# First four tiles of the first layer as fp32 products, and a last batch pooled with queries on the partitions

## The reference

```python
# layer 0, per batch, with the expert of the batch
h = gelu(x @ fc1_w.T + fc1_b)                     # 512 -> 2048, exact gelu
y = concat([h @ fc2_w.T + fc2_b,                  # 384 shared outputs
            h @ experts_w[idx].T + experts_b[idx]])  # 128 outputs of the expert
x = x + y
# layer 1
s = tanh(x @ W1 + b1) @ v                         # one score per token
# mask by the batch's type: l <= j, l >= j, or l != j
p = softmax(where(mask, s[None, :], -1e30), -1)   # 512 x 512
x = x + (p @ x) / mask.sum(-1)[:, None]
```

## Time and profile before

| what | us |
|---|---|
| median of three runs | 1385.22 |
| profiled execution | 1384.67 |
| its span, first to last instruction | 1382.8 |
| TensorE busy | 1355.1 (98%) |
| VectorE busy | 1208.0 (87%) |
| ScalarE busy | 853.2 (62%) |
| SP's queue of DMAs | 61.90 MB, 13.3% of 16 engines |

### The profile page before, as it was taken

The page is one execution under the profiler, slowest core; times in us unless marked ns, Lnnn a source line. Parts: engine busy times, 40 slices in busy tenths (PEclk is TensorE's granted clock), DMA queues, the critical chain, the costliest instruction groups (busy, mean ns, idle before and its releaser), DMA issues.

```text
span 1382.8 us, 21714 instructions
## 1 busy us (share of the span) xinstructions
PE 1355.1 (98%) x8666; PEld 862.6 (62%) x8666; DVE 1208.0 (87%) x2025; ACT 853.2 (62%) x1471; POOL 0.2 (0%) x4
## 2 busy tenths in 40 slices
PE   6989999999999999999999999999999999999997
PEld 2437658485675847557484665847567484765855
DVE  6788589988888988889988888988889898888998
ACT  4776837568383765828467483765928467483753
POOL 0000000000000000000000000000000000000000
PEclk9999999999999999999999999999999999999999
DMA  7141002020100202001020200202011020200001
GB/s 257 36 178 62 1 23 69 1 84 9 62 31 16 78 1 77 16 31 62 9 84 1 69 24 16 77 0 77 16 46 48 16 77 1 77 16 16 16 18 46
DMA packets 29623, 63.82 MB, mean 46 GB/s; under 512 B 5970, under 2 KB 6610, under 8 KB 27090
## 3 DMA queue, kind: packets, MB, share of 16 engines
q1 hardware_dynamic: 29090, 61.90, 13.3%
q10 hardware_dynamic: 432, 0.53, 0.1%
HBM read 45.64 MB, written 16.78 MB: 45 GB/s over the span
## 4 chain that ended last, share of the span: by engine, by line
PE 92%; DVE 4%; ACT 2%; issue 0%; DVEq 0%
PE ps L469 44%; PE ps L398 40%; PE ps L485 4%; PE ps L351 2%; DVE raw L160 1%; PE ps L493 1%; ACT hh L169 1%; PE ps L666 1%; ACT w2h L169 1%; DVE cl L166 0%; ACT xl L1004 0%; DVE w1l L166 0%; DVE xr L160 0%; PE ps L776 0%; DVE raw L509 0%
## 5 line engine op out<-in xcount | busy, mean ns | idle before, releaser
L469 PE MATMUL ps<-hh,w2h 128*128 128x512 f16 x768 | 291.8, 380 | 0.0
L469 PE MATMUL ps<-hh,w2l 128*128 128x512 f16 x768 | 291.8, 380 | 0.0
L469 PE MATMUL ps<-hl,w2h 128*128 128x512 f16 x768 | 291.6, 380 | 0.0
L398 PE MATMUL ps<-xh,w1h 128*128 128x256 f16 x960 | 261.7, 273 | 0.3 <-DVE xl L166 0.3
L398 PE MATMUL ps<-xl,w1h 128*128 128x256 f16 x960 | 261.7, 273 | 0.0
L398 PE MATMUL ps<-xh,w1l 128*128 128x256 f16 x960 | 261.7, 273 | 0.0
L441 ACT ACTIVATE g<-ps,b1s,ds 128x512 f32<-128x512 f32 x240 | 173.9, 775 | 101.6 <-PE ps L398 101.6
L160 DVE TENSOR_TENSOR raw<-raw 128x512 f32<-128x512 f32 (+2 forms) x324 | 219.9, 699 | 1.0 <-issue 0.2
L509 DVE TENSOR_TENSOR_SCAN raw<-raw 128x512 f32<-128x512 f32 x180 | 213.2, 1213 | 0.0
L398 PE MATMUL ps<-xh,ch 128*128 128x256 f16 x720 | 196.4, 273 | 0.0
L398 PE MATMUL ps<-xl,ch 128*128 128x256 f16 x720 | 196.3, 273 | 0.0
(11 more groups left out here) (162 smaller groups left out, 2009.5 us busy)
## 6 DMA issues: line engine op xcount, KB each, us to landing
out<-xr SPq DMA_DIRECT2D x63, 256.0 KB, 2.4
xr<-in_xT SPq DMA_DIRECT2D x62, 256.0 KB, 2.9
er<-in_ew SPq DMA_DIRECT2D x15, 1024.0 KB, 5.6
raw<-in_w SPq DMA_DIRECT2D x32, 256.0 KB, 7.7
er<-in_w SPq DMA_DIRECT2D x3, 1024.0 KB, 10.1
xr<-in_ew SPq DMA_DIRECT2D x1, 1024.0 KB, 5.7
xr<-in_xT ACTq DMA_DIRECT2D x2, 256.0 KB, 4.8
aws<-in_aw SPq DMA_DIRECT2D x1, 256.0 KB, 8.6
```

The costliest lines, as they stand in the source:

```text
L398: r = e.matmul(half_bank(*to), w, m, start=i in (1, 5) and c == 0 and n == 0, stop=c == 1 and n == 2, skip_group_check=True)
L469: m = e.matmul(out_bank, w, h[:, k, :], start=False, stop=k == NH - 1 and i == 2, skip_group_check=True)
```

## The change

Start of batch 0:

- Tiles 0 to 3 of the first layer are computed as fp32 products of unsplit w1 and x (`plain`), in an order by arrival; their GELUs take scale 1.0 and write to `g` and not over w1. 36 small products on ones precede everything. Bounds of w1 tiles 0 to 5 and x are taken before the first scale; those of tiles 6 to 9 come behind the low parts of x.
- The splits of w1 tiles 0 to 3, which later batches need, move behind tiles 5 and 6 and to output block 0. w1 tiles 4 to 15 are reloaded one by one in the loop, tiles 0 to 3 not at all; x of batch 1 is loaded before the loop. h parts 0 and 1 are made before the loop. The bound of w2's second block moves into the loop, the expert's bound and scale from output block 1 to block 0, w2's third bound to (0, 2). The load of w2's third block is issued last.

Last batch:

- The pooling of batch 14 stops ahead of the last four operations of its last block; they are issued behind the weights' sum.
- Scans read the scores in PSUM, without the masks' constants, which are added in the two following maxima; one masked copy of the scores is left, and its second half waits for a scan.
- x (natural layout) is copied once more, unsplit, to `xn`. In the products the weights are stationary and nh, nl moving: queries are on the partitions, and the output is in token layout, put in order on the host side together with the transposition that was there. The fourth query tile is in two pieces of 256 columns.
- Totals: three adds of the four weight rows on VectorE, then four one-column fp32 products; count, product and reciprocal are 128x4. Evacuation is one operation per piece. Idle products: 17 and not 22.

```diff
+    def plain(k, cs=range(KD)):
+        if 0 in cs:
+            bank_of[k] = turn()
+        n, free = bank_of[k]
+        for c in cs:
+            fc1_done[0, k] = PE.op(lambda e, c=c: e.matmul(pf[n], w1r[k][:, c * P:(c + 1) * P], xr[:, 0, c, :], start=c == 0, stop=c == KD - 1),
+                                   w1_ready[k], x_ready[0, c], *free)
...
+    warm(36)
     w1_biggest(0)
     biggest(x5[:, 0, 0:1], xr[:, 0, 0, :], x_ready[0, 0])
     w1_biggest(1)
...
+    w1_biggest(2, 3, 4, 5)
+    w_max = w1_column(0, 3)
...
     def first_batch():
-        fc1(0)
+        for k, cs in ((0, (0, 1)), (1, (0, 1)), (0, (2, 3)), (1, (2, 3)), (2, (0, 1, 2))):
+            plain(k, cs)
+        sx_ready[0] = t = chain_scale(xc(0), w1c + 3, chain_sum(xc(0), w1c + 3, w_max, x_max))
+        plain(2, (3,))
+        plain(3)
+        fc1_scale(0, 2, 3, t)
+        split_w1_high(4, t)
+        x_hi = [split_x0_high(0)]
         gelu(0)
+        x_hi += [split_x0_high(c) for c in (1, 2, 3)]
         gelu(1)
+        split_w1_high(5, t)
+        gelu(2)
+        split_x0_low(0, x_hi[0])
         split_w1_low(4)
+        for c in (1, 2, 3):
+            split_x0_low(c, x_hi[c])
+        w1_biggest(6, 7, 8, 9)
+        first["pairs"] = t
         t = w1_column(3, 5)
         gelu(3)
         fc1(4, (0, 1))
         summed = chain_sum(w1c + 3, w1c + 5, t)
...
-        done = 0
+        for j in (0, 1):
+            high(0, j)
+            low(0, j)
+        for c in range(KD):
+            load_x(1, c)
+        done = 2
...
+                reload_w1([j] if j >= PLAIN else [])
             done += 2
             if k >= 12:
                 split_w2(0, 0, k - 12)
-        load_w2(2, 0, w2s_ready[0, 3])
-        big = one_bound(w2c + 1, 0, er[:, 1, :], w2_ready[1])
+            if k == 14:
+                big = one_bound(w2c + 1, 0, er[:, 1, :], w2_ready[1])
...
+        load_w2(2, 0, w2s_ready[0, 3])
...
+        if (o, j) == (0, 0):
+            first["expert"] = one_bound(ec(0), 2, expert_rows(0), e_ready[0])
...
-            reload_w1(range(NH // 2, NH))
+        if (o, j) == (0, 2):
+            first["sum"] = chain_sum(ec(0), ec(0) + 1, first["expert"])
+            expert_scale(0, chain_scale(ec(0), ec(0) + 1, first["sum"]))
             first["big"] = one_bound(w2c + 2, 1, er[:, 0, :], w2_ready[2])
+            for k in (2, 3):
+                split_w1_high(k, first["pairs"])
+                split_w1_low(k)
...
-            first["big"] = one_bound(ec(0), 2, expert_rows(0), e_ready[0])
```

```diff
+            if c == KD - 1:
+                yield HELD
...
+    def own_scores(b, v, *waits):
+        n, half, done = half_s[v]
+        emptied[n] = AC.op(lambda e: e.activation(sc[:, HALVES[v]], half, ACT.Identity, bias=cS[:, b:b + 1]), done, s_free[b - 1], *waits)
+        return emptied[n]
...
+        return DV.op(scan(o, mF[:, 0:1].broadcast_to([P, S // 2]), d, start, ALU.max, ALU.max), done, *waits)
...
+        maxF = scan_half(mF, 1, False, first_max)
+        t = scan_half(mB, 1, True)
+        own_second = own_scores(b, 1, t)
         scol_ready = AC.op(copy_column, scol_done)
+        maxB = scan_half(mB, 0, False, t)
+        m1 = DV.op(stt(mt, mFx, cF[:, i], sc, ALU.add, ALU.max), maxF, own_first, own_second)
+        m2 = DV.op(stt(mt, mBx, cB[:, i], mt, ALU.add, ALU.max), m1, maxB)
...
         weight_low(3)
+        s01 = DV.op(tt(be, row[0], row[1], ALU.add), wh_ready[1])
+        s23 = DV.op(tt(mt, row[2], row[3], ALU.add), wh_ready[3])
+        summed = DV.op(tt(be, be, mt, ALU.add), s01, s23)
+        count_last = DV.op(ts(rz[:, :], lcol[:, :], cntq[:, i], cntp[:, i], ALU.mult, ALU.add))
+        finish()
...
+        def product(piece, t, n):
+            q, d, target, free = piece
+            x, w = ((nh, ph), (nl, ph), (nh, pl))[n]
...
+        for piece in pieces:
+            for n in range(3):
+                p = product(piece, 3, n)
+            q, d, target, _ = piece
+            o = DV.op(stt(xn[:, q, d], target[:, d], rz[:, q:q + 1], xn[:, q, d], ALU.mult, ALU.add), p, r)
+            stored[b, q] = SP.dma(load(out[b, :, q, d], xn[:, q, d]), x_out[b % XB * KD + q], o)
...
-    finish()
-    ones_ready = DV.op(lambda e: e.memset(ones[:, :].bitcast(f32), 1.0), fc1_end[b])
+    finish(hold=True)
+    own_first = own_scores(b, 0)
+    first_max = scan_half(mF, 0, True, own_first)
     evacuate_half(b, 1)
     attend_half(b, 1)
```

More of the change, by code:

```diff
@@ L11 @@
 XB = 3
-GR = 4
+GR = PLAIN = 4
 PAIRS = NH // 2
@@ L613, in fill, with finish @@
                 credit[0] -= cost * 0.92
-    def finish():
+    def finish(hold=False):
         for p in pools:
-            for _ in p:
-                pass
+            for cost in p:
+                if hold and cost == HELD:
+                    return
         pools.clear()
     pen = xr[:, (B - XB) % XB, :, :]
-    seen, nat_ready = {}, {}
+    seen, nat_high, nat_ready = {}, {}, {}
     def see(b, t):
@@ L645, in natural_up @@
             done = PE.op(fn, *free, eye_ready, ready[v])
-        n3 = nh[:, :, c * P:(c + 1) * P]
-        return n, lambda: AC.op(lambda e: e.activation(n3, pf[n].rearrange("p (a b) -> p a b", a=4), ACT.Copy), done, fc1_end[b])
+        bank4 = pf[n].rearrange("p (a b) -> p a b", a=4)
+        parts = [(t[:, :, c * P:(c + 1) * P], done, ready) for t, ready in ((nh, fc1_end[b]), (xn, es_ready[b, 3]))]
+        return n, [lambda part=part: AC.op(copy(part[0], bank4), *part[1:]) for part in parts]
     def natural_low(b, c, n, high):
@@ L760, in pool_last @@
         bank_z, free_z = turned[2]
[L761 to L802, removed]
+        pieces = [(q, slice(0, S), pf[n], free) for q, (n, free) in enumerate(turned[:2])]
@@ new lines, in pool_last @@
+        pieces += [(2, slice(0, S), po(b, 2), (half_x2[1],)), (3, HALVES[0], pa, (half_tanh[1],)), (3, HALVES[1], bank[7], free_of[7])]
+        def product(piece, t, n):
+            q, d, target, free = piece
+            x, w = ((nh, ph), (nl, ph), (nh, pl))[n]
+            waits = (ph_ready[t], nat_high[3]) if n == 0 else (ph_ready[t], nat_ready[3]) if n == 1 else (w_ready[t],)
+            return PE.op(lambda e: e.matmul(target[:, d], w[:, t, q * P:(q + 1) * P], x[:, t, d], start=t == 0 and n == 0, stop=t == 3 and n == 2), *waits, *free)
@@ new lines, in pool_last, with totals @@
+        for n in range(3):
+            for piece in pieces:
+                product(piece, 0, n)
+        for t in (1, 2):
+            for piece in pieces:
+                for n in range(3):
+                    product(piece, t, n)
+        def totals(e):
+            for q in range(4):
+                m = e.matmul(pf[bank_z][:, q:q + 1], be[:, q * P:(q + 1) * P], ones[:, :], start=True, stop=True)
+            return m
+        z = PE.op(totals, summed, ones_ready, *free_z)
+        z3 = DV.op(tt(rz[:, :], pf[bank_z][:, 0:4], rz[:, :], ALU.mult), z, count_last)
@@ L806, in build @@
+        r = DV.op(lambda e: e.reciprocal(rz[:, :], rz[:, :]), z3)
+        for piece in pieces:
+            for n in range(3):
+                p = product(piece, 3, n)
+            q, d, target, _ = piece
+            o = DV.op(stt(xn[:, q, d], target[:, d], rz[:, q:q + 1], xn[:, q, d], ALU.mult, ALU.add), p, r)
+            stored[b, q] = SP.dma(load(out[b, :, q, d], xn[:, q, d]), x_out[b % XB * KD + q], o)
     for c in (0, 1):
@@ L874, in set_bits, with warm, fn @@
         return PE.op(fn, oneb_ready)
+    def warm(count):
+        def fn(e):
+            for n in range(count):
+                m = e.matmul(pss[:, 0:P], oneb[:, :], oneb[:, :], start=True, stop=True)
+            return m
+        PE.op(fn, oneb_ready)
     for n in (4, 6):
@@ L940, in first_batch @@
         gelu(5)
+        split_w1_high(0, first["pairs"])
+        split_w1_low(0)
         split_w1_high(8, t)
@@ L948, in first_batch @@
         gelu(6)
+        split_w1_high(1, first["pairs"])
+        split_w1_low(1)
         fc1(7, (0, 1, 2))
@@ L978, in first_batch @@
                 seed(0, 0)
-            for j in range(done, done + 2):
+            for j in range(done, min(done + 2, NH)):
                 high(0, j)
                 low(0, j)
+                reload_w1([j] if j >= PLAIN else [])
             done += 2
@@ L1339 @@
     got = r.results[0]["out"]
-    return c(got.transpose(0, 3, 2, 1)).reshape(B, S, D)
+    y = c(got.transpose(0, 3, 2, 1)).reshape(B, S, D)
+    y[B - 1] = got[B - 1].transpose(1, 0, 2).reshape(S, D)
+    return y
```

109 lines of the change are left out of this document (32 added, 77 removed).

## The result

The changed kernel takes 1381.47 us (median of nine runs, 1380.17 to 1382.11), the kernel before 1384.60 (nine runs, 1383.88 to 1385.81). The ratio is 0.9977, with a 95% interval of 0.9968 to 0.9985: 3.1 us faster, where 7.4 were forecast. The time lies in the predicted range at its upper end, beyond the forecast's own range. It is 3.7 above the forecast and not 4.3, because the forecast started from the median of three runs, 1385.22, and nine give 1384.60. The profiled execution took 1381.64 us, its span is 1379.9.

What follows compares the result with a forecast made beforehand. TensorE, full through the middle, was taken as the bound, so only the ends could gain: 2.9 us (start) + 4.5 (tail) = 7.4; 1384.67 became 1377.3, plus 0.55 for the median: 1377.8 us. Own range 1375.8 to 1379.8, outer 1373.8 to 1381.6.

Steps and rivals of the forecast that it cites:

- 2.9 us gained: Start: batch 1's first product comes at 108.9 instead of 111.81, passing one to one through the full middle.
- (a): Start, tiles 0 to 3: fp32 products cost TensorE 3.4 us more but begin early; chain sum 15.45, tile 3 done 19.85.
- D: Rival, start: fp32 products run at the lower clock, making the kernel 3.7 us slower, 1388.9; chance 0.04.
- (b): Start: TensorE waits 3.5 us at the chain sum until 24.95, then 1.4 us lost to a clock fall.
- Rival A: Start: the clock doesn't fall in the new waits, batch 1 starts 1.4 + 1.0 earlier, 1375.4; chance 0.17.
- (c): Start, GELU 11 (47.9) to the second output block's seed: ScalarE bounds, ending at 70.4 against 71.2; TensorE waits 2.3.
- (d): Start, after 70.4: the moved w2 bound brings batch 1's scale to 85.5 against 88.09, 2.6 gained.
- rival B: Start: late last w2 block or a VectorE hole swallows the front gain; only the tail left, 1380.7; chance 0.15.
- Has until 70.4 (cover: 6.2 us): Start: w2's last block, 1 MB, loads from 64.2 behind w1 reloads on SP's queue, with 6.2 us before needed.
- (e) to (g): Tail: earlier first weight (1361.0), products until 1374.9, short reciprocal and one-step evacuations until 1375.6; 4.5 us gained with stores.
- C: Rival, tail: narrow pieces are bound by weight loads and stores queue; tail gains 3.0, 1379.3; chance 0.10.
- The stores: Tail end: last stores lie 0.7 to 0.4 us apart instead of 1.3 to 0.7, costing 0.2 us.

Runs made afterwards that it cites:

- e1: Kernel before with only the diff's batch 0 hunks, last batch as before: 1384.75 us, ratio 1.0000 to the kernel before.
- e4: Changed kernel with w2's first block's last split and w2's third block's load ahead of the last two h parts and w1 reloads: 1379.22 us.
- e7: Changed kernel with batch 14's last four pooling operations issued before the last batch's scans, nothing held back: 1384.18 us, ratio 1.0004 to the kernel before.
- e9: Changed kernel without the stores of the last batch's first two query tiles: 1380.88 us, ratio 0.9973 to the kernel before.
- e5: Changed kernel with 54 small products on ones ahead of the chain sum at 25.4, filling TensorE's wait: 1379.17 us.
- e6: e5 with 50 more small products ahead of batch 1's three-column chain sum: 1378.80 us, ratio 0.9960 to the kernel before.
- e2: Kernel before with only the diff's last-batch hunks, start as before: 1381.11 us, ratio 0.9976 to the kernel before.
- e3: Changed kernel with the bounds of w1 tiles 6 to 9 and their column moved ahead of the first scale: 1376.15 us.
- e10: Changed kernel without the 36 small products on ones at the start: 1382.41 us, ratio 0.9986 to the kernel before.
- e8: Changed kernel with e3 and e4 together, and the moved bound's squares each given its own buffer: 1374.04 us.
- e11: e8 with the masks' VectorE operations issued at the first instead of a later second-layer block: 1373.96 us, ratio 0.9925 to the kernel before.
- e12: e11 with 54 small products on ones ahead of the three-column chain sum: 1372.38 us, ratio 0.9913 to the kernel before.

## Why the prediction was wrong

The sign, the places and most mechanisms were right; the size was not, 3.1 us against 7.4. The part that failed is the start's "2.9 us gained": there is no gain (e1), and 0.55 us of loss in the profiled execution. That the time still lies in the outer range, 1373.8 to 1381.6, is in part luck: with the base of 1385.22 the same gain would give 1382.1.

**(a) held.** Chain sum at 15.86 (forecast 15.45), tile 3 done at about 20.3 (19.85), as full speed came at 7.3 and not at 6.0. Eleven profiles with the 36 small products have this chain sum at 15.43 to 15.86, a spread of under half of the 1 us that the prediction gave it. D is out. (In D's sum, the stretch from tile 9 to batch 1 gains 0.5 by (b) and (d), 2.9 less 2.4, not 0.2; nothing else hangs on it.)

**(b) held, in most executions.** The wait was forecast at 3.5 us until 24.95 and is 3.30 until 25.40. The fall's "1.4 us lost" was 1.4 to 1.7 in five profiles (9.86 to 10.13, less 8.44) and 2.7 in the one after. What failed there was the spread that I gave it, none. The 1.4 stands for a low stretch of 3.4 us, as seen before; after, it was 6.8. GELU 11, forecast at 47.9, is at 47.92 to 48.39 in e1, e4, e7 and e9, and at 49.51 after. Rival A, no fall, is out: no profile with this wait is without it, but for e5 and e6, where products fill it.

**(c), (d) are what failed in every execution, and in rival B's way.** Forecast were 37.6 us from GELU 11 to batch 1's scale; it takes 39.4 after, and 39.4 to 39.7 in e1, e7 and e9. "Has until 70.4 (cover: 6.2 us)" is the failed step: the prediction put the wait for this load at nothing, and ScalarE waits 1.2 to 1.5 us for it. The load of w2's last block was issued 17.0 us after GELU 11, at 66.53 and not 64.2, as the last split of w2's first block, behind the last h splits, ends at 66.50 and frees the buffer only then: I had looked at SP's queue alone. And it takes 7.1 us, where 4.9 in e4 would have fitted. That is 1.25 of the 1.8 missed (e4); 0.4 more are the squares of the moved bound, which wait for each other. B's point, "from 3 us later than 70.4", was met at 73.60 in the profile after; in e1 and e7 the load lands at 72.8 and 72.4, and the start gains only 0.3 and 0.6 there (batch 1 at 111.52 and 111.17, before 111.81). B's outcome, only the tail left, is what e1 and e2 show. From the scale to the first product forecast and trace agree, 23.4.

In sum the start missed 3.46 in the profiled execution: 0.45 by (a), 1.2 by the long fall, 1.8 by the load and squares. In e1, with the short fall, it missed 2.6: 0.5 until GELU 11, and 2.1 by the load and squares.

**(e) to (g) held.** First weight 6.25 us after the evacuation (6.0), last evacuation 20.92 (20.6): C's slow narrow pieces are not there, their products lie 0.12 us apart (0.114 forecast). The scans out of PSUM cost what the forecast gave them, three halves in 2.10. The own scores, in turn with them, end at 1360.09, before the maxima start at 1360.22, and cost nothing, as forecast.

**The stores did not.** They give back 1.0 instead of 0.2, by which the tail brings 3.4 in the trace (e2: 3.3 by the ratio, 0.0024 x 1384.6), not 4.5. Only 0.35 has a shown cause. The Trainium skill (DMA: Bandwidth & Descriptors, "Latency and other measured facts") puts a DMA's fixed time down to the memory's round trip, which grows with load. The trace agrees in direction: the last store lands 2.7 us after its issue, 2.4 with two stores fewer, 1.9 in the kernel before, where they lay further apart.

Open stay the last 0.65 us of the stores, and what sets the length of a clock fall behind the same wait, 3.4 or 6.8 us.

## What to carry to other kernels

Price a new wait of TensorE with the slow stretch behind it: here that was 1.6 or 2.5 us behind a wait of 3.3, and differs between executions. Before moving work, look for an engine that idles earlier and could take a later stage's bounds there: one column of bounds moved so (e3) gave more than the whole change. For a load that is moved, work out its issue anew from the work that frees its buffer, not from its queue alone. Where two bounds lie nearly level, an experiment that removes one shows nothing; remove both before calling either harmless.

## What was unexpected in the hardware

- Behind the same wait of 3.3 us the low stretch was 6.8 us long in the profile after (24.0 to 30.9, from inside the wait) and 3.4 in five others, whether it began in the wait (e9 at 24.6, e10 at 26.2) or behind it (e1, e4 and e7, at 26.0 to 26.3). The second fall had the same two lengths: 3.4 in after, e1, e3, e4, e5, e7 and e8, 6.8 in e9, e10 and e11. No length between was seen at these two places. The Trainium skill (TensorE: Matmul & The Clock Gate, "What's actually happening") says that activity releases the throttle at a point that varies from run to run; these executions agree.
- Small products on ones in the wait kept the granted clock at 1.00 (e5, e12), and without a fall the times spread less: 0.1 us over five runs of e12, 0.7 and 0.9 over five each of e8 and e11.
- A 1 MB load took 4.9 us issued ahead of the last reloads (e4), and 7.0 to 7.7 behind them (after, e1, e5, e7).
- An fp32 product of 512 columns takes 0.86 us for its two records from 7.3 on, right behind the small products; without them (e10) 1.8 for the first ones. A 128x512 reciprocal is 3.35 us and a 128x4 one 0.18.
